# Asking for x ahead of the gate rows, and spreading the first statistics of an AdaLN block over the pair steps

## The reference, cut to what matters

```
mod = (silu(c) @ wmod) -> sa, ca, ga, sb, cb, gb          # six rows of 128 for each batch
ga, gb = sign * max(|.|, 0.25)
h = layernorm(x) * (1 + ca) + sa
x = x + ga * attention(h)      # linear attention with elu+1, a fixed memory, causal in 128 tokens
h = layernorm(x) * (1 + cb) + sb
x = x + gb * moe(h)            # 8 experts, top 2, gelu, 128 -> 512 -> 128
```

## Time and profile before

| | |
|---|---|
| median of 3 runs | 572.16 us (571.8 to 572.68) |
| the profiled execution | 572.52 us, its span 570.8 us |
| mean granted TensorE clock | 0.842 of full speed |
| busy share of the span | PE 67%, DVE 79%, ACT 58%, POOL 55% |
| chain that ended last | PE 39%, DVE 27%, POOL 14%, issue 10% |

### The profile page before, as it was taken

How to read it: one execution, slowest core, us unless ns; L and a number is a source line. 1 busy time by engine, 2 the same in 40 slices (tenths; PEclk the granted TensorE clock), 3 DMA queues, 4 the chain that set the end, 5 groups by cost and what they waited for, 6 DMA issues and landing times.

```text
span 570.8 us, 14921 instructions
## 1 busy us (share of the span) xinstructions
PE 382.1 (67%) x4184; PEld 339.5 (59%) x4185; DVE 450.4 (79%) x1081; ACT 331.5 (58%) x746; POOL 312.9 (55%) x344
## 2 busy tenths in 40 slices
PE   3551646874377646626999999999999999930000
PEld 3341545764276535514998999999898898930000
DVE  4659888888888888755888888988999999975213
ACT  1432547896188836424666667767666666694211
POOL 2248200000277777777777500077878878788671
PEclk9997768788587876856999999999999999985555
DMA  3499101526154751812474433455555555566231
GB/s 108 130 316 358 39 1 32 164 73 196 41 165 133 234 155 52 233 55 79 115 147 138 130 99 95 100 130 143 129 143 133 133 134 137 123 172 168 60 84 53
DMA packets 129681, 73.19 MB, mean 128 GB/s; under 512 B 53745, under 2 KB 122993, under 8 KB 129393
## 3 DMA queue, kind: packets, MB, share of 16 engines
q1 hardware_dynamic: 121456, 56.02, 35.3%
q0 software_dynamic: 8192, 16.79, 11.1%
HBM read 21.75 MB, written 34.90 MB: 99 GB/s over the span
## 4 chain that ended last, share of the span: by engine, by line
PE 39%; DVE 27%; POOL 14%; issue 10%; ACT 4%; DMA 3%; DVEq 2%; ACTq 0%; SPq 0%
PE psA L1149 16%; POOL ROW L493 14%; PE psA L1137 8%; PE psV L1137 4%; PE psH L1137 4%; DVE ATT L747 3%; PE psH L1047 3%; DVE X L816 2%; DMA X<-in_x 2%; DVE stats L690 2%; DVE stats L823 2%; DVE w_bound L926 2%; ACT HH L580 1%; ACT ATT L574 1%; DVE AM L778 1%
## 5 line engine op out<-in xcount | busy, mean ns | idle before, releaser
L482 POOL DMA_INDIRECT slot_rows<-ROW,POS x128 | 132.4, 1034 | 114.3 <-DVE EXPT L901 75.9
L493 POOL DMA_INDIRECT ROW<-slot_out,POS x128 | 147.0, 1148 | 86.6 <-DMA slot_out<-VP 48.1
L1149 PE MATMUL psA<-WST,ATT 128*128 x2040 | 139.1, 221 | 2.0 <-DVE VP L970 1.6
L1149 PEld LDWEIGHTS psA<-WST,ATT 128*128 128x128 f16 x2040 | 125.0, 98 | 12.3 <-issue 3.6
L961 DVE SCALAR_TENSOR_TENSOR ATT<-ATT,f_scales 128x1024 f16<-128x1024 f32 x85 | 109.1, 1284 | 3.0
L635 ACT ACTIVATE ATT<-psA,b1T,f_scales 128x256 f32<-128x256 f32 x172 | 83.1, 563 | 36.0 <-PE psA L1137 35.2
L959 DVE TENSOR_SCALAR ATT<-ATT,f_scales 128x1024 f16<-128x1024 f32 x85 | 65.2, 768 | 22.6 <-ACT ATT L635 21.2
L1137 PE MATMUL psA<-WT,WST 128*128 128x256 f16 x516 | 65.7, 279 | 5.9 <-DVE RT L889 3.7
L635 ACT ACTIVATE ATT<-psV,b1T,f_scales 128x256 f32<-128x256 f32 x84 | 42.9, 561 | 37.1 <-PE psH L1137 33.2
L1137 PEld LDWEIGHTS psA<-WT,WST 128*128 x516 | 48.4, 99 | 13.9 <-issue 6.6
L1047 PE MATMUL psH<-ident,ATT 128*128 128x128 f32 x64 | 15.2, 380 | 57.7 <-DVE ATT L747 57.7
(11 more groups left out here) (200 smaller groups left out, 721.5 us busy)
## 6 DMA issues: line engine op xcount, KB each, us to landing
slot_out<-VP SPq DMA_DIRECT2D x85, 128.0 KB
slot_rows<-zero SPq DMA_DIRECT2D x9, 1024.0 KB, 5.8
X<-in_x SPq DMA_DIRECT2D x8, 512.0 KB, 7.8
WST<-in_W SPq DMA_DIRECT2D x2, 2048.0 KB, 11.8
WST<-WT SPq DMA_DIRECT2D x16, 256.0 KB, 2.3
out<-X SPq DMA_DIRECT2D x16, 256.0 KB, 2.4
slot_rows<-ROW,POS POOLq DMA_INDIRECT x128
GA<-gate_rows SPq DMA_DIRECT2D x1, 2048.0 KB, 11.4
```

Source lines behind the costliest of these rows:

```text
L482: nc.gpsimd.indirect_dma_start(xg[g], bass.IndirectOffsetOnAxis(ap=POS[:, k * TILES + t:k * TILES + t + 1], axis=0), ROW[:, t * 2 * D:(t + ...
L493: nc.gpsimd.indirect_dma_start(YG[:, o:o + D], None, yg[g], bass.IndirectOffsetOnAxis(ap=POS[:, i:i + 1], axis=0)).then_inc(gathered[c % 2 ...
L1149: last = mm(psD[k % 2][:, h * D:(h + 1) * D], a[:, k % 2, i:i + TOK], W2S[:, ds(e * 2 * FF + b * FF + m * D, D)], start=(m == 0 and c == 0 ...
```

## The change

The six late loads of x move ahead of the gate transfers on SP. Clearing `MEMO` moves from POOL to VectorE, and the wait for it goes. The statistics of lot 0 move ahead of the wait for the modulation. The 40 tiles of lot 2 are cut into 16 (after step 1) and 24 (after step 2). `scales` moves from after step -1 to after step 1, and the refinement of lot 2, the weight bounds and the weight scales move one step on. ACT's part of the last two lots moves one step on, too. On PE the spreading of the gate rows moves from ahead of step -1 to behind it, and the wait for the routing constants moves into `route`.

```diff
@@ SP
-            sp.dma_start(Xv[:, 8:16, :], xt[:, 8:16, :]).then_inc(x_in[1], 16)
+            for n in range(1, 8):
+                sp.dma_start(Xv[:, 8 * n:8 * n + 8, :], xt[:, 8 * n:8 * n + 8, :]).then_inc(x_in[n], 16)
...
-            for n in range(2, 8):
-                sp.dma_start(Xv[:, 8 * n:8 * n + 8, :], xt[:, 8 * n:8 * n + 8, :]).then_inc(x_in[n], 16)
@@ POOL
-            nc.gpsimd.memset(MEMO[:], 0.0).then_inc(const_ready, 1)
@@ ACT
-            steps(act, step, route, {0: lambda: first_norm(1), 1: lambda: first_norm(2), 3: lambda: act.wait_ge(ln1_ready, 3)},
+            steps(act, step, route, {0: lambda: first_norm(1), 2: lambda: first_norm(2), 4: lambda: act.wait_ge(ln1_ready, 3)},
@@ DVE
             nc.vector.tensor_tensor(c_silu[:], cT[:], c_den[:], ALU.mult).then_inc(silu_ready, 1)
+            link(nc.vector.memset(MEMO[:], 0.0))
...
-            def statistics(n):
-
-                a, b = LN1[n:n + 2]
+            def tiles(a, b):
+
                 for t in range(a, b):
                     if t % 8 == 0:
                         dve.wait_ge(x_in[t // 8], 16)
                     last = nc.vector.bn_stats(stats1[:, t * 6:t * 6 + 6], X[:, t * D:t * D + D])
-                link(last)
+                return last
+
+            def statistics(n, done=0):
+
+                a, b = LN1[n:n + 2]
+                link(tiles(max(a, done), b))
...
+            statistics(0)
             dve.wait_ge(mod_mm, 1)
...
-            statistics(0)
             refine(0)
...
-            dve.wait_ge(const_ready, 5)
...
-            def other_statistics():
+            SECOND_HALF = 40
+
+            def second_statistics():
                 statistics(1)
                 refine(1)
 
-            def last_statistics():
+            def bounds_and_tiles():
+                scales()
+                tiles(LN1[2], SECOND_HALF)
+
+            def last_refine():
                 refine(2)
                 weight_bounds()
 
-            steps(dve, step, route, {-1: scales, 0: other_statistics, 1: lambda: statistics(2), 2: last_statistics, 3: weight_scales}, weights=True)
+            steps(dve, step, route, {0: second_statistics, 1: bounds_and_tiles, 2: lambda: statistics(2, SECOND_HALF), 3: last_refine, 4: weight_scales}, weights=True)
@@ PE
-            pe.wait_ge(gr_ready, 1)
-            for b in range(2 * EARLY):
-                last = mm(psH[:, b * D:(b + 1) * D], ident[0:BATCH, b:b + 1].broadcast_to([BATCH, 128]), gate_pair[:, 0:D],
-                          start=True, stop=True)
-            last.then_inc(ga_mm, 1)
+
+            def first_gates():
+
+                pe.wait_ge(gr_ready, 1)
+                for b in range(2 * EARLY):
+                    last = mm(psH[:, b * D:(b + 1) * D], ident[0:BATCH, b:b + 1].broadcast_to([BATCH, 128]), gate_pair[:, 0:D],
+                              start=True, stop=True)
+                last.then_inc(ga_mm, 1)
...
                         pe.wait_ge(mod_ready, 1)
-                        pe.wait_ge(route_const, GROUPS + 1)
...
             def route(g):
 
+                pe.wait_ge(route_const, GROUPS + 1)
...
-            steps(pe, step, route)
+            steps(pe, step, route, {-1: first_gates})
```

## The result

The changed kernel takes 564.16 us (median of 4, 563.96 to 564.41), against 571.98 for the kernel before on the same occasion: ratio 0.9866, 95% interval 0.9848 to 0.9885, so 6.6 to 8.7 us less. The forecast was 563.4. The profiled executions, which the sum was made for, went from 572.52 to 564.06 us (spans 570.8 to 562.3): 8.5 less, where 9.1 was forecast. By the medians the gain is 7.8, and the interval above doesn't reach 9.1: the time was met, the gain was forecast somewhat too large.

A forecast was written before the change was run, and what follows sets the result against it. VectorE's queue was taken to bound the edited early stage. 12.9 us gained at the start, less 0.5 for stalls and 3.3 given back, makes 9.1: 572.5 becomes 563.4 us, range 559 to 569.

The forecast's parts named there:

- VectorE's queue sets the end of this stage: Stage before the matmul stretch from 300 us: what leaves VectorE's queue or fills its idle time counts.
- The memset is hidden: Start, VectorE: the new memset of MEMO takes 2.2 us, ends at 5.9, before x's first load lands at 6.24.
- refine(0) at 11.15: Start, VectorE: ends at 11.15 against 16.59; 5.4 us from 3.2 of statistics and moments moved, and the 2.80 us mean.
- Step 1 at 24.7: Lot 1's statistics end at 24.7 instead of 37.56: 12.9 us gained at step 1's start, less 0.5 for POOL stalls.
- 3.3 given back between steps 1 and 5: VectorE's queue takes 62.4 us instead of 59.1: scales adds 2.35, POOL's folding reaching into step 3 adds 0.9.
- x lands by 20, the fold is covered: Loads and POOL: x about 20, GA about 31, fold starts 36 to 38.5, 6 to 8 us spare before step 2.
- Lumps are worth nothing: Steps 1 to 5: cutting the lumps doesn't shorten them, since ACT and PE wait for VectorE in either order.
- Everything behind step 5 moves as a block: Scatters, experts and gathers wait on their predecessors, so 9.1 us gained at step 5 stays to the end.
- only part comes through: First 30 us: code loads, POOL stalls and full queues take more; 6.5 to 3 us gained, 566 to 569.5; chance 0.16.
- More than forecast: Steps 2 and 3: shorter PE pauses bring a faster clock, and POOL's fold ends early; 557 to 560.5 us; chance 0.13.
- Rival 3: Step 2 stands for the fold because GA comes late; first fold later than about 54, 575.4 us; chance 0.04.
- Rival 4: Behind step 5: a later stage sets the end by itself, gain given back, 571 to 573.2 us; chance 0.05.

The follow-up runs named there:

- short_fold: The changed kernel with POOL's fold multiplying 2 of each batch's 128 columns, leaving out part of the computation: 559.99 us, ratio 0.9798.
- fill: The changed kernel with statistics tiles, and the weight scales, moved into VectorE's idle time, and lot 2's moments behind step 3: 558.34 us, ratio 0.9760.
- u_stats0: The changed kernel with the statistics of lot 0 again behind the modulation: 568.45 us, ratio 0.9938.
- w_late: The changed kernel with SP waiting for the first fold before it asks for W1 and W2: 564.76 us, ratio 0.9867.
- u_gates: The changed kernel with PE's gate matmuls again ahead of the first transposes: 566.74 us, ratio 0.9906.
- u_mem: The changed kernel with MEMO cleared by POOL again: 564.55 us, ratio 0.9873.
- fill_ga: fill with only batches 4 to 7 of GA loaded ahead of the first fold, the rest of GA, W1 and W2 after it: 557.63 us, ratio 0.9762.
- u_lumps: The changed kernel with lot 2 again in one lump of 40 tiles, its refinement, bounds and weight scales placed as before: 564.65 us, ratio 0.9876.
- x_only: The kernel before with one part of the change alone, all of x asked for ahead of the gate transfers: 567.70 us, ratio 0.9913.
- u_x: The changed kernel with x[2] to x[7] again asked for behind the two gate transfers: 570.09 us, ratio 0.9972.

## Why the prediction was right, step by step

1. *VectorE's queue sets the end of this stage.* Right, and shown twice: taking away stalls (short_fold) and filling holes (fill) came out at the end with nearly their full size.
2. *The memset is hidden.* Right: 1.78 us plus 0.38 of issue for an estimated 2.2, over before x[0] lands. The 2.2 does not follow from the row named for it, 0.69 us for 512 elements, which in proportion gives 2.8; as the memset is hidden, nothing hung on it.
3. *refine(0) at 11.15.* It ended at 11.14. What it consists of was right in the main: the statistics in their old place cost 3.2 us here (u_stats0, +4.1 at the end), and the stall of `mean` is the rest. But of the 3.2 us of work about 1 still runs past 8.22, where the modulation is ready. In return VectorE's wait for ACT's rstd, 0.52 us in the kernel before, is gone, since the modulation's operations now stand in it.
4. *First transposes at 12.9, QK at 16.1.* 12.92 and 15.94. The identities came at 11.5, not late.
5. *Step 1 at 24.7, with 0.5 taken off for stalls of the gate operations, so 12.4 gained.* 24.31, 13.2 gained. The stall was next to nothing: L722 took 0.35 us, and 0.28 (w_late) to 0.62 (u_gates) in the other runs without the long memset. By the rule of the Trainium skill that the prediction weighed the 0.5 would have been nearly 0, and it was; with POOL's long memset in place the one operation that it names took 1.92 us (u_mem). The other 0.3 are lot 1, 6.0 us from 18.32 on for 6.2 from 18.5 on.
6. *3.3 given back between steps 1 and 5.* This term was too small: 4.4. From 24.31 to 87.85 are 63.5 us, not 62.4. `scales` took 2.2 of the 2.35 expected. Step 3 took 11.2 us (55.78 to 66.97) where it took 9.3: 1.3 for the norms beside POOL, as expected, and 0.6 for a wait for ACT and slower operations of the `rstd` refinement, which step 2 had before. Step 2 got 0.6 shorter in return (10.9 for 11.5). The moments of lot 2 took 3.2 us, 2.7 before and 2.8 in the sum. Steps 4 and the weight scales added 0.35. I had allowed 0.9 for all of this, and 2.1 came. The 0.8 too little at the start of step 1 and the 1.1 too little given back here nearly cancel. That the sum came within 0.4 of the 8.7 gained at step 5 is in part luck.
7. *x lands by 20, the fold is covered.* The effect was right, the reasons in part wrong. The gate rows landed at 21.0 (21.5 expected), 5.6 us after their issue instead of 1.5, and GA at 31.2. The all-reduce did not suffer from x's traffic: 6.26 us, where I allowed 10.7. The pause ahead of the fold got longer, 13.2 us, and that GA's traffic stretches it was found only by the runs, in one trace without that traffic (fill_ga). The cover held: the V matmuls of step 2 began at 44.24, the first fold ended at 38.0.
8. *Lumps are worth nothing.* Right as far as the medians can tell (u_lumps, +0.6 +-1.5). So cutting lot 2, one of the changes, had no part in the gain that these runs can show.
9. *Everything behind step 5 moves as a block.* Right: 8.7 at step 5, 8.4 at the last pair step, 8.5 at the end.

Of the rivals, "only part comes through" was nearest. Its place for a loss, `scales` waiting for the all-reduce, did not occur, but would have with `scales` left where it was. "More than forecast" by a faster clock did not happen: the granted clock over the whole run was 0.840 for 0.842 before, and in the pause of the weight bounds it fell as before (0.56 from 70 to 80 us, 0.62 before). Rival 3 needed a first fold behind 54, and it began at 36.25. Rival 4 is out, as nothing behind step 5 gave anything back.

The six undone parts add up to 17.8 us, more than twice the gain. They stand behind each other. `scales` in its old place meets a wait of 4.69 us where it was 2.48 in the kernel before, and a late x one of 8.19 where it was 3.29. Each fix makes the next wait longer, so a single one can look smaller alone than in the set: x_only moved step 1 by 4.1, u_x by 8.4. Only x was tried alone; for the other parts this is argued from the waits.

## What to carry to other kernels

Where one engine's queue sets the end of a stage, replay that queue on a clock with the durations of the trace: at each wait take the later of "queue free" and "data there". Here each stretch came out within 1.1 us, and the sum within 0.4. Then look at what the earlier start will ask for sooner, and at the remaining waits as places for work that has no deadline: short, independent operations such as `bn_stats` went into them almost without delaying anybody (`fill`). Cutting such work into lumps did nothing by itself (`u_lumps`); it paid where the pieces landed in a wait.

## What the runs showed of the hardware

- A VectorE tensor_scalar from SBUF to SBUF stands for POOL: 2.80 (`mean`, before) and 1.92 us (L722, u_mem) beside POOL's memset of 1.82 and the short ones behind it, against 0.17 (changed kernel) and 0.28 (w_late); four norms 2.39 beside the fold, 1.11 to 1.18 without it. A scalar_tensor_tensor with both inputs in SBUF and two operations that read PSUM, beside the same memset, kept their 0.40 to 0.41 (u_mem).
- POOL's pause behind the all-reduce, ahead of its first ordinary tensor_tensor, was 7.56 us with the queues nearly empty (fill_ga), 9.02 with x and W1 but no longer GA in flight (u_x), 10.75 in the kernel before, and 11.6 to 13.9 in the other eleven runs, all with GA in flight. It ends 4.0 to 6.1 us behind GA's landing in all of them but u_x. What in GA's traffic does it is open. x's load (DMA share 0.69 over that pause) left the pause ahead of the all-reduce at 6.26, while with GA and x in flight (u_x, share 0.89) the all-reduce came only at 27.59, 11.45 us after POOL's last operation. That the pause is the loading of code is read from the MODIFY_POOL_CONFIG at its start, not measured apart.
